# Affinities issued earlier and projections one body ahead in the graph stage of a three-stage kernel

## The reference, cut to what matters

```python
def _gat_attention(self_feat, cond_adj, label_bias, Wq, bq, Wk, bk, Wout, bout):
    kv = self_feat[:, :20]
    qh = (self_feat @ Wq.T + bq).reshape(B, N, 16, 8)
    kh = (kv @ Wk.T + bk).reshape(B, 20, 16, 8)
    aff = jnp.einsum('bnhd,bmhd->bnhm', qh, kh) * (1.0 / np.sqrt(8))
    aff = jnp.where(cond_adj[:, :, None, :] > 0, aff, NEG) + label_bias[:, :, None, :]
    w = jax.nn.softmax(aff, axis=-1)
    out_t = jnp.einsum('bnhm,bmf->bnhf', w, kv)
    out = jnp.einsum('bnhf,hgf->bnhg', out_t, Wout) + bout.reshape(16, 8)
    return out.reshape(B, N, F)

row_zero = v.sum(-1) == 0
q_exp = jnp.where(row_zero[..., None], 0.0, q[:, None, :])
self_feat = jnp.concatenate([v, q_exp], axis=-1) @ W_self.T + b_self
output = self_feat                 # plus _gat_attention for d = 0 and d = 1
result = v + jax.nn.relu(output)
```

## Time and profile before

| | us |
|---|---|
| median of 3 runs | 737.24 (734.24 to 740.25) |
| the profiled execution | 738.05, its span 736.60 |
| attention, until the first feed-forward matmul | about 459 |
| feed-forward, until the first graph matmuls | about 520 |
| graph, until the end of the span | 736.60 |

### The profile page before, as it was taken

How to read it: one execution, slowest core, us unless ns; L and a number is a source line. 1 busy time by engine, 2 the same in 40 slices (tenths; PEclk the granted TensorE clock), 3 DMA queues, 4 the chain that set the end, 5 groups by cost and what they waited for, 6 DMA issues and landing times. The chain is left out here.

```text
span 736.6 us, 17167 instructions
## 1 busy us (share of the span) xinstructions
PE 659.2 (89%) x5496; PEld 570.5 (77%) x5496; DVE 468.8 (64%) x1010; ACT 477.6 (65%) x1707; POOL 337.4 (46%) x390
## 2 busy tenths in 40 slices
PE   5789999999999999999999985999789898988874
PEld 5578888888888888888888874899667777777763
DVE  4456666666765666666676555576266776768672
ACT  4767877887797797788779771688344444444541
POOL 1334354445444435344444344466426564655642
PEclk9989999999999999999999999799789999999995
DMA  7212012021011102202201210234111111111100
GB/s 230 57 25 54 16 53 60 7 61 53 25 42 53 51 17 53 58 9 60 53 20 40 54 41 18 71 112 126 54 47 29 52 37 50 39 53 42 30 15 29
DMA packets 57757, 36.77 MB, mean 50 GB/s; under 512 B 15536, under 2 KB 54480, under 8 KB 57728
## 3 DMA queue, kind: packets, MB, share of 16 engines
q1 hardware_dynamic: 54480, 27.80, 13.8%
q0 software_dynamic: 3248, 8.61, 3.8%
HBM read 30.05 MB, written 6.34 MB: 49 GB/s over the span
## 5 line engine op out<-in xcount | busy, mean ns | idle before, releaser
L477 POOL TENSOR_TENSOR p<-p,p_rsum 128x512 f32<-128x512 f32 x128 | 130.4, 1040 | 126.3 <-DVE p_rsum L793 126.3
L694 ACT ACTIVATE p<-banks,neg_max 128x128 f32<-128x128 f32 x512 | 182.4, 393 | 0.1
L672 ACT ACTIVATE wide<-banks 128x512 f32<-128x512 f32 x128 | 78.3, 612 | 73.9 <-PE banks L530 71.3
L694 ACT ACTIVATION_READ_ACCUMULATOR p<-banks,neg_max 128x1 f32 x512 | 120.2, 235 | 0.0
L804 DVE COPY oT<-banks 128x512 f32<-128x512 f32 x64 | 44.1, 689 | 78.3 <-PE banks L581 78.3
L566 PE MATMUL banks<-ident,p 128*128 128x128 f32 x512 | 75.4, 281 | 17.5 <-DVE oT L804 15.3
L786 DVE TENSOR_REDUCE neg_max<-banks 128x8 f32<-128x1024 f32 x64 | 77.6, 1212 | 17.7 <-PE banks L555 16.3
L528 PE MATMUL banks<-xT_hi,w_qkv_hi 128*128 128x256 f32 x256 | 83.9, 328 | 4.0 <-DVE w_qkv_lo L196 2.5
L566 PEld LDWEIGHTS banks<-ident,p 128*128 128x128 f32 x512 | 56.2, 142 | 26.4 <-issue 17.3
L555 PE MATMUL banks<-wide 64*128 64x128 f32 x1024 | 74.4, 285 | 0.2 <-ACT wide L672 0.2
L529 PE MATMUL banks<-xT_lo,w_qkv_hi 128*128 128x256 f32 x256 | 74.1, 290 | 0.0
(11 more groups left out here) (147 smaller groups left out, 1474.5 us busy)
## 6 DMA issues: line engine op xcount, KB each, us to landing
early<-in_mask SPq DMA_DIRECT2D x16, 220.0 KB
early<-in_mask SPq DMA_DIRECT2D x80, 44.0 KB
x_in<-in_x SPq DMA_DIRECT2D x16, 128.0 KB, 2.2
x_gb<-in_x SPq DMA_DIRECT2D x16, 128.0 KB, 2.2
gate_msa<-rows_scratch SPq DMA_DIRECT2D x16, 128.0 KB, 3.0
gate_b_out<-rows_scratch SPq DMA_DIRECT2D x16, 128.0 KB, 3.4
f_x_in<-x_scratch SPq DMA_DIRECT2D x16, 128.0 KB, 2.4
f_x_res<-x_scratch POOLq DMA_DIRECT2D x16, 128.0 KB, 2.8
```

What stands on the lines that cost most here:

```text
L477: pool.tensor_tensor(p[:, par, heads, :], p[:, par, heads, :], p_rsum[:, par, heads].unsqueeze(2).broadcast_to([128, 4, T]), ALU.mult).the ...
L672: act.activation(dst, proj_ps[k % 2], ACT.Copy).then_inc(proj_saved[k % 2], 1)
L694: act.activation(p[:, par, m, :], s_ps[par][:, e, j, :], ACT.Exp, bias=neg_max[:, par, 4 * e + j:4 * e + j + 1], accum_out=p_sum[:, par, m ...
```

## The change

- TensorE's body is now: affinity(s,1), turn_w(s,0), values(s+1,0), turn_x(s+2), weights_v(s,0), self_features(s+2), affinity(s+1,0), turn_w(s,1), values(s+1,1), turn_self(s+2), weights_v(s,1), keys(s+2), queries(s+2). So affinities stand ahead of the transposes that need an exponential, and keys and queries are one body ahead. The queries' buffer is doubled for it, and ScalarE saves keys and queries at the start of its body.
- VectorE's body is: bias, maximum and subtraction of (s,1); reciprocal and `save_out` of (s,0); `save_v(s+1,0)`; self terms of s+2; bias, maximum and subtraction of (s+1,0); reciprocal and `save_out` of (s,1); `save_v(s+1,1)`; `finish(s-1)`.
- The self terms: the row sums are taken in the feed-forward stage, after the result is there; the conditioning row times the test is added to the self features in one pass per batch, straight from PSUM. b_self comes in elsewhere: as a bias where ScalarE saves the turned self features, and in the constant that GpSimd adds (one more addition in `set_constants`, one more load of 128 numbers in the setup).
- ScalarE's `copy_keys` follows `save_selfT` directly. SP's loads of the graph stage wait for the saved self features instead of the self terms.

```diff
@@ feed-forward, vector
+        def sum_rows(s):
+            at = bass.ds(s.n * 2, 2) if not isinstance(s.n, int) else slice(2 * s.n, 2 * s.n + 2)
+            dve.wait_ge(x2_ready, s.n + 1)
+            dve.reduce_sum(g.row_sums[:, at], x2[:, s.par], AX.X).then_inc(g.rows_summed, 1)
...
+            if more(s, -2):
+                sum_rows(step_from(s, -2))
@@ graph, tensor
-            if nxt:
-                keys(step_from(s, 1))
             if here:
+                affinity(s, 1)
                 turn_w(s, 0)
-                affinity(s, 1)
-            if nxt:
-                queries(step_from(s, 1))
+            if nxt:
+                values(step_from(s, 1), 0)
...
+            if nxt:
+                affinity(step_from(s, 1), 0)
             if here:
                 turn_w(s, 1)
             if nxt:
-                affinity(step_from(s, 1), 0)
                 values(step_from(s, 1), 1)
             if second:
                 turn_self(step_from(s, 2))
             if here:
                 weights_v(s, 1)
+            if second:
+                keys(step_from(s, 2))
+                queries(step_from(s, 2))
@@ graph, vector
+            for b in range(2):
+                last = dve.scalar_tensor_tensor(out=self_nat[:, s.par, b, :], in0=q_row[:, s.par, b, :],
+                                                scalar=nonzero[:, b:b + 1], in1=src[:, b * D:b * D + D],
+                                                op0=ALU.mult, op1=ALU.add)
...
-            if more(s, -1):
-                invert_sums(step_from(s, -1), 1)
-                save_out(step_from(s, -1), 1)
             if here:
                 add_bias(s, 1)
                 shift_scores(s, 1)
...
+                add_bias(step_from(s, 1), 0)
+                shift_scores(step_from(s, 1), 0)
             if here:
+                invert_sums(s, 1)
+                save_out(s, 1)
+            if nxt:
+                save_v(step_from(s, 1), 1)
@@ setup and constants
-KEPT = 11
+KEPT = 12
+                (g.b_selfT[:], a["b_self"].rearrange("(p o) -> p o", o=1)),
+        dve.tensor_tensor(b_gsum[:], b_gsum[:], g.b_self[:], ALU.add).then_inc(consts_set, 1)
```

More of the change, by code:

```diff
@@ L1353, in body @@
                 done = step_from(s, 2)
-                sp.wait_ge(self_add_ready, done.n * 2 + 2)
+                wait_saved(sp, done, SELF)
                 load(step_from(s, 4))
@@ L1474, in affinity @@
             for d in range(2):
-                last = pe.matmul(aff_ps[b][:, d].rearrange("p h m -> p (h m)"), qT[:, d, b, :],
+                last = pe.matmul(aff_ps[b][:, d].rearrange("p h m -> p (h m)"), qT[:, s.par, d, b, :],
                                  k_block[:, s.par, b, d].rearrange("p h m -> p (h m)"), start=True, stop=True)
@@ L1505, in body @@
             here, nxt, second = more(s, 0), more(s, 1), more(s, 2)
+            if here:
+                affinity(s, 1)
+                turn_w(s, 0)
             if nxt:
-                keys(step_from(s, 1))
-            if here:
-                turn_w(s, 0)
-                affinity(s, 1)
-            if nxt:
-                queries(step_from(s, 1))
+                values(step_from(s, 1), 0)
             if second:
@@ L1517, in body @@
                 weights_v(s, 0)
-            if nxt:
-                values(step_from(s, 1), 0)
             if second:
                 self_features(step_from(s, 2))
+            if nxt:
+                affinity(step_from(s, 1), 0)
             if here:
@@ L1538, in tensor @@
         pe.wait_ge(consts_set, 1)
+        keys(zero)
+        queries(zero)
         run_bodies(pe, body)
@@ L1548, in save_selfT @@
             src, saved = wait_full(act, s, SELFT)
-            act.activation(selfT[:].rearrange("p b t -> p (b t)"), src[:, 0:2 * T], ACT.Copy).then_inc(saved, 1)
+            act.activation(selfT[:].rearrange("p b t -> p (b t)"), src[:, 0:2 * T], ACT.Identity,
+                           bias=g.b_selfT[:]).then_inc(saved, 1)
         def copy_keys(s):
@@ L1559, in save_q @@
             for d in range(2):
-                last = act.activation(qT[:, d].rearrange("p b t -> p (b t)"), src[:, d * 2 * T:d * 2 * T + 2 * T],
+                last = act.activation(qT[:, s.par, d].rearrange("p b t -> p (b t)"), src[:, d * 2 * T:d * 2 * T + 2 * T],
                                       ACT.Identity, bias=q_bias[:, d:d + 1], scale=GSCALE)
@@ L1608, in body @@
                 save_selfT(step_from(s, 2))
+                copy_keys(step_from(s, 2))
             if nxt:
@@ L1614, in scalar @@
             save_selfT(zero)
+            copy_keys(zero)
             return
@@ L1619, in vector, with save_self @@
     def vector(dve, first=False):
-        def sum_rows(s):
-            dve.wait_ge(x_loaded[s.par], s.half * 16 + 16)
-            dve.reduce_sum(row_sum[:], x_in[:, s.par], AX.X).then_inc(summed, 1)
         def find_nonzero(s):
-            dve.wait_ge(summed, s.n + 1)
-            dve.tensor_scalar(nonzero[:], row_sum[:], 0.0, None, ALU.not_equal).then_inc(nonzero_ready, 1)
-        def add_self_terms(s):
+            at = bass.ds(s.n * 2, 2) if not isinstance(s.n, int) else slice(2 * s.n, 2 * s.n + 2)
+            dve.wait_ge(g.rows_summed, s.n + 1)
+            dve.tensor_scalar(nonzero[:], g.row_sums[:, at], 0.0, None, ALU.not_equal).then_inc(nonzero_ready, 1)
+        def save_self(s):
             dve.wait_ge(nonzero_ready, s.n + 1)
             dve.wait_ge(q_row_loaded[s.par], s.half * 16 + 16)
-            for b in range(2):
-                dve.scalar_tensor_tensor(out=self_add[:, b, :], in0=q_row[:, s.par, b, :],
-                                         scalar=nonzero[:, b:b + 1], in1=g.b_self[:], op0=ALU.mult,
-                                         op1=ALU.add).then_inc(self_add_ready, 1)
-        def save_self(s):
-            dve.wait_ge(self_add_ready, s.n * 2 + 2)
             zero_wait(dve, self_b_ready, s.n - 1)
             src, saved = wait_full(dve, s, SELF)
-            dve.tensor_tensor(self_nat[:, s.par], src[:, 0:2 * D].rearrange("p (b f) -> p b f", b=2), self_add[:],
-                              ALU.add).then_inc(saved, 1)
+            for b in range(2):
+                last = dve.scalar_tensor_tensor(out=self_nat[:, s.par, b, :], in0=q_row[:, s.par, b, :],
+                                                scalar=nonzero[:, b:b + 1], in1=src[:, b * D:b * D + D],
+                                                op0=ALU.mult, op1=ALU.add)
+            last.then_inc(saved, 1)
         def save_v(s, b):
@@ L1695, in body @@
                 shift_scores(s, 1)
-            if second:
-                sum_rows(step_from(s, 2))
-            if here:
                 invert_sums(s, 0)
+                save_out(s, 0)
             if nxt:
@@ L1704, in body @@
                 find_nonzero(step_from(s, 2))
-            if here:
-                save_out(s, 0)
-            if second:
-                add_self_terms(step_from(s, 2))
                 save_self(step_from(s, 2))
@@ L1711, in body @@
                 add_bias(step_from(s, 1), 0)
+                shift_scores(step_from(s, 1), 0)
+            if here:
+                invert_sums(s, 1)
+                save_out(s, 1)
+            if nxt:
                 save_v(step_from(s, 1), 1)
-                shift_scores(step_from(s, 1), 0)
             if more(s, -1):
@@ L1761, in build @@
         g.b_self = sb("b_self_sb", [128, D])
+        g.b_selfT = sb("b_selfT_sb", [128, 1])
+        g.row_sums = sb("row_sums", [128, B])
+        g.rows_summed = ctx.enter_context(nc.semaphore("rows_summed"))
         g.gqk_w = sb("gqk_w", [128, 4, D])
```

17 lines of the change are left out of this document (5 added, 12 removed).

## The result

| | before | after |
|---|---|---|
| median | 735.74 us (4 runs, 733.89 to 740.25) | 765.77 us (4 runs, 760.92 to 767.06) |
| ratio, 95% interval | | 1.039 (1.034 to 1.044) |
| profiled execution | 738.05, span 736.60 | 765.28, span 763.8 |

The changed kernel is 3.9% slower. The forecast was 759, with a range of 744 to 768.

A forecast was written before the change was run, and what follows sets the result against it. Neither engine alone bounds the graph stage: TensorE and VectorE wait for each other once a body. 738.05 + 21.6 (bodies) + 0.3 + 0.2 + 1.0 - 1.5 = 759.7, forecast as 759 us, range 744 to 768.

The forecast's parts named there:

- Steps 1 to 5: The walk along the queues through one changed graph-stage body: 12.0 us at full clock instead of 11.14.
- step 5: Keys, ScalarE's copy, queries and affinity of b=1 follow `save_v` one after another, to 11.99 us.
- A spell in nearly every body: Graph stage: TensorE's longer idle stretch brings low clock in nearly every body, 1.44 us each.
- rivals without spells (739): No graph-stage body has a low-clock spell any more: 2.0 us more for 14 bodies, 739; chance 0.10.
- with one in two (749): Low-clock spells in every second graph-stage body, as before: 12.7 us a body, 749; chance 0.18.
- rival of 707: Path over the keys' bank shorter than reckoned, so halves of 4.83 us show: 707; chance 0.06.
- step 4: End of TensorE's body: keys wait for `save_v`, now behind reciprocal and `save_out`; TensorE stands about 1.4 us.
- +0.3 of the constants: One more 128x128 addition in `set_constants`, on the path between the first two stages: +0.3 us.
- +0.2 of the first pair: Very first pair: two self-term passes stand on the path where one did, +0.2 us.
- range of 752 to 767: The forecast's own range, 0.4 us on a body each way; chance 0.58.
- what would show it: Signs expected in the profile after: TensorE waits for `g_v_block` about 1.3 us, `g_kT` about 0.6; full-clock bodies 12.0 apart.
- step 2: Affinity of b=0 goes ahead of `turn_w`; VectorE's `save_v`, test and self passes fit the gap of 1.4 us.

The follow-up runs named there:

- Experiment 1: Five unused 128x128 matmuls added to the kernel after, where TensorE stands waiting for `save_v` before the keys: 740.98 us, ratio 1.006.
- Experiments 2: The kernel after, with the keys given their own PSUM columns in another bank: 728.55 us, ratio 0.988.
- experiments 3: The kernel after, with `save_v` of b=1 put back between bias and maximum of b=0: 743.84 us, ratio 1.014.
- experiment 4: Parts each alone on the kernel before: self terms 735.74 us; keys and queries one body ahead 767.35 us; affinities ahead of `turn_w`, outputs saved behind subtractions 733.71 us.
- experiment 5: The kernel before, with affinities ahead of `turn_w`, outputs saved behind subtractions and the new self terms, without the projections ahead: 722.72 us, ratio 0.984.
- experiment 6: The kernel after, with only the queries moved back behind the affinity of b=1, keys staying ahead: 758.88 us, ratio 1.031.

## Why the forecast was right, and where its size was off

**Steps 1 to 5 held.** Experiment 1 shows the body without its spell: 12.06 against the 11.99 worked out. Its parts too: the half from b=1 to b=0 takes 4.82 (4.83), TensorE stands 1.25 before the keys (1.4), 0.57 before the queries, and queries to the next `turn_w` are 2.04. Experiments 2 and 3 confirm the causes that steps 4 and 5 name: with the bank of the keys split off the body is 10.86, with `save_v` early the kernel gains 2.5%. What step 5 lacks is ScalarE's order: where the keys come early, their copy waits for the exponential (experiments 3 and 4). In the kernel after that costs nothing, since `save_v` holds the keys back until the exponential is over.

**The clock held in kind.** "A spell in nearly every body" was 14 of 14 (fewer than 8 would have refuted it). The rivals without spells (739) and with one in two (749) fall with it; experiment 1, at 741, is what the first of them would have looked like. The rival of 707 needed a path over the bank of under 1.7 us beyond `save_out`; from the end of `save_out` (623.27) to the affinity (625.84) it is 2.6 in experiment 1.

**The sum, term by term**, between the starts of `add_bias` of b=1, where the two traces can be laid side by side:

| stretch | before | after | difference | forecast |
|---|---|---|---|---|
| up to the first keys | 528.23 | 525.72 | -2.5 | +0.3 |
| first keys to the first such addition | 15.38 | 17.92 | +2.5 | +1.2 |
| 14 bodies | 164.43 | 192.43 | +28.0 | +21.6 |
| the next one | 12.20 | 9.73 | -2.5 | -1.5 |
| to the end of the span | 16.35 | 18.00 | +1.7 | 0 |
| sum | | | +27.2 | +21.6 |

*The bodies, +28.0 for +21.6.* This is the term that was mis-sized, and it has several small causes, each times 14. The spell costs 13.65 - 12.06 = 1.59, not the 1.44 taken over from before: 2.1. Before, the rows of a spell from start to start are longer by 1.68 in all, of which 1.44 reach the body; now all 1.59 of queries and affinity do, while VectorE is idle. I had said so ("both on the path") and still carried over the old price. The first four bodies are 14.17, 14.07, 13.87 and 13.73 long instead of 13.65: 1.2. About half of that is not the clock, since the first four bodies of experiment 1 are 12.16 to 12.23 long instead of 12.06 at full clock; the cause of the rest stays open. The path is 12.06 for 11.99, and I rounded 13.43 down to 13.4: 1.4 together. And the old loop, cut at the additions, has bodies of 11.745 and not 11.86: 1.6.

*The edges.* In the first body the keys of pair 1 wait 2.42 us for `save_v`, and behind that wait four query records take 2.08 where 1.13 is the time at full clock: the walk of the loop (step 4) holds there too, and I had costed that body at +1 by its order alone. The last body but one gains 2.5, because what it sheds in the old loop was a long one (12.2), not the 11.14 that I subtracted from. At the end +1.7, for which I had no term. A lower clock isn't the reason: from the start of `turn_w` of the last pair but one (706.05 and 735.87) to the end the granted clock is 0.74 before and after. The rows of GpSimd behind the last saved output, which ends at 728.49 before and at 754.39 after, show most of it. Before:

```profile
728.58 0.71 POOL L1380 TENSOR_TENSOR g_o_sum<-g_o 128x256 f32<-128x256 f32 x1 [3.71 <-DVE g_o L1675]
```

And after:

```profile
755.02 0.73 POOL L1402 DMA_DIRECT2D out<-g_y  x1 [5.96 <-DVE g_y L1688]
755.77 0.73 POOL L1388 TENSOR_TENSOR g_o_sum<-g_o 128x256 f32<-128x256 f32 x1
```

`finish` of the pair before now stands behind the last `save_out`, so its store comes first in GpSimd's queue, and the sum starts 1.38 instead of 0.09 behind the saved output: 1.3 of the 1.7. The -2.5 ahead of the graph stage lie mostly in the attention stage (the first feed-forward matmul starts at 459.45 before and at 457.21 after), whose matmuls the change doesn't touch. I take them for scatter between executions: in the twelve traces here that start lies between 457.2 and 459.7. They hid a little more than the 2 us that the edges missed, so the 759 is nearer to 766 than its parts deserve.

**The small terms.** The timeline of VectorE in the feed-forward stage after (L1170 the residual, L1176 the row sums):

```profile
494.30 0.42 DVE L1170 TENSOR_TENSOR f_x<-banks,f_x_res 128x256 f32<-128x256 f32 x1 [0.62 <-PE banks L1068]
...
496.04 0.41 DVE L1176 TENSOR_REDUCE row_sums<-f_x 128x256 f32 x1
```

The row sums cost nothing, as their term said: the wait before the residual is 0.62 here where it was 0.83, and the stage's pitch of 3.58 us per pair is unchanged. Experiment 4 gives all the self terms as 1.000 on the kernel before, to within 0.3% or some 2 us; the +0.3 of the constants and the +0.2 of the first pair are too small to be seen there, and no run shows them by themselves. My own range of 752 to 767, which the result is in, is 0.5 us on a body each way and not 0.4.

**One thing in "what would show it" was wrong.** I wrote that VectorE's wait for the affinity of b=0 would be 1.3 and for b=1 3.1. The first is 0.2 to 0.4 of idle time: 1.3 is the gap, and `save_v`, the test and the self passes fill it, as step 2 itself said. The second is 3.30 at full clock (experiment 1) and 4.87 with a spell.

## What to carry to other kernels

Before an operation is moved to fill a gap, ask which buffer it writes and who empties it last: here the projections were put into a gap of TensorE, but their half bank was emptied by a pass of VectorE that the same change had moved behind two others, and by a copy on ScalarE that comes behind an exponential. With the projections ahead alone, where only the second holds, the kernel is as slow as with the whole change (experiment 4); an order of ScalarE with the copy first stays untested. A wait that stands at the end of an in-order queue is paid by all behind it. And a part of a change that measures nothing alone (the self terms) can be worth over 1% once another part has made its engine the bound, so parts are to be timed together as well as apart.

## What the runs showed of the hardware

- Waits of 0.8 to 1.7 us between groups of small matmuls are often followed, though not each time (every second time before the change), by stretches at 1.2 instead of 2.4 GHz; four or five unused matmuls in the wait took them all away, for 3.3% in the kernel after, 1.6% in the one before and 1.3% in that of experiment 5. The Trainium skill ("TensorE: Matmul & The Clock Gate", section "HAM oscillation — how this bites in real kernels") puts the falls down to much longer gaps; the runs here don't agree. Its section "A second HAM failure mode: psum-queue depth-cycling" does describe short ones, and they do.
- The price of such a spell isn't fixed: 1.44 us before and 1.59 after, by what stands in it.
- Bodies with a spell last 13.63 to 14.17 us in the kernel after, 13.35 to 13.73 in 12 of the 14 of experiment 6, and 13.1 to 14.6 with the projections ahead alone. What sets these lengths is open.
- A pass over 128x2 elements on VectorE can take 0.73 us instead of 0.16 beside an addition on GpSimd (experiment 5), and two passes over 128x128 1.14 instead of 0.61 (experiment 4).
